# Routing of two expert layers in a five-stage model kernel: GpSimd takes choices, products and table rows, and ranks are handed on by halves

## The chip, the cores and the metric

The kernel runs on 1 core of one Trainium2 chip. The metric is the device time of one execution in microseconds (us); smaller is better. The engines are TensorE (PE, with weight loads PEld), VectorE (DVE), ScalarE (ACT), GpSimd (POOL) and SyncE (SP), which here only issues DMA. They run their own instruction streams and meet at semaphores.

## The reference, cut to what matters

The model is two layers of cross attention, a mixer (a state-space scan, then self attention) and an expert layer, on T = 2048 tokens of 256 values. The change is in the routing of the two expert layers, so that is what is shown. Layer 0 has 64 experts, 6 choices a token, a capacity of 128 tokens an expert; layer 1 has 64 experts in 8 groups, 8 choices a token, no capacity.

```python
# layer 0
scores = jax.nn.softmax(xf @ gate_w.T, axis=-1)
_, idx = jax.lax.top_k(scores + gate_b, K)            # K = 6
flat_e = idx.reshape(-1); order = jnp.argsort(flat_e); se = flat_e[order]
counts = jnp.bincount(flat_e, length=E); starts = jnp.cumsum(counts) - counts
pos = jnp.arange(T * K) - starts[se]                  # a token's rank in its expert
xb = jnp.zeros((E, CAP, D), xf.dtype).at[se, pos].set(xf[tok], mode='drop')
...
# layer 1
scores = jax.nn.sigmoid(x @ w_router); swb = scores + b_router
group_scores = jnp.sum(jax.lax.top_k(swb.reshape(..., 8, 8), 2)[0], axis=-1)
group_idx = jax.lax.top_k(group_scores, 4)[1]
masked_scores = jnp.where(mask, swb, 0.0)
topk_idx = jax.lax.top_k(masked_scores, 8)[1]
sort = jnp.argsort(idx_flat); x_sorted = x_flat[sort // TOPK]
```

Each layer then runs every expert's gated product on its tokens, and adds a shared expert that all tokens pass.

## The kernel before, in words

`stage_moe` is called for layer 0 (`capped`) and for layer 1. Each call has a block for routing (prefix `m0r_`, `m1r_`), and then a block for the experts (`m0x_`, `m1x_`), with a barrier between them. The tokens lie as 16 tiles of 128 partitions; a half is 8 tiles (`HN`).

The steps of the routing block, nearly all on DVE, each waiting for the one before:

1. `normed`: 16 normalised tiles into the ring `xr` (4 buffers), stored to memory by SP and turned by PE; `logits` follow on PE. The ring's buffer is free when its store has landed.
2. `chosen(0)`, `chosen(1)`: per half the scores, the best 6 or 8 experts (`MAX8`, `FIND_INDEX8`), their numbers as floats `topf`, and for each choice k a one-hot row `oh` (L1418, 128 x 8 x 64, one instruction).
3. ranks: PE multiplies every `oh` with a triangular matrix and with ones (L1299, 2 matmuls for each k and half, sums in `psl`, `pst`). It waits for `hs` of the first shared units, and signals once, at the end of both halves.
4. DVE runs the sum over 16 tiles (`before`, L1441, a chain) and adds `psl` into `sel` (L1442). Layer 1 adds the start of each expert's block (L1446 to L1453).
5. slots: for each half K products `oh * sel` (L1462) and a reduction (L1464). Between them DVE gates units of the shared expert (L1169), for which PE (`units`, L1154) makes the products and ACT the SiLU. In layer 0 seven units are made in this block, in layer 1 four. PE starts unit m only when `hs` of unit m - 2 is written (two PSUM buffers).
6. the table: for each token tile and choice, n = 0 to 95 or 127, a one-hot row `atp` of the slot (L1483), a row `atb` (the token's number at its expert or block; L1486 or L1488 on DVE, L1346 or L1352 and L1354 on ACT), and one matmul (L1313). `by_scalar(n)` says which `atb` ACT makes: in layer 0 two of three, in layer 1 one of three. A ring of 16 (`HQ`) joins them. ACT comes to its rows only after its last SiLU.
7. `tok` and `dest` are read from the table; the barrier; the experts start with indirect gathers on POOL.

POOL has nothing to do in the routing block. The order on each engine is that of the code.

## Time and profile before

| | us |
|---|---|
| median of 3 runs | 2326.88 (2324.38 to 2330.84) |
| the profiled execution | 2326.39 |
| its span | 2324.7 |
| routing of layer 0, by the trace | 829.7 to 925 |
| routing of layer 1, by the trace | 1650.6 to 1791.6 |

Busy shares over the whole span are PE 80%, DVE 67%, POOL 54%, ACT 45%. They are averages over stages with different limits: in both routing stretches POOL's row of the page's 40 slices is 0, and DVE's is at its highest. The page's chain that ended last follows the last stage's gathers and stores and names none of the routing lines, because it is followed back along one release at a time; the barrier behind each routing block makes all engines wait for it.

### The profile page before, as it was taken

The numbers are of one execution on the slowest core, as the hardware profiler recorded it, in microseconds if no ns is written. First come the engines' busy times: TensorE is split into PE (matmuls) and PEld (weight loads), VectorE is DVE, ScalarE is ACT, GpSimd is POOL, SyncE is SP. The second block draws the span as 40 slices with busy tenths as digits, with TensorE's granted clock in tenths as the row PEclk, the third lists the DMA queues.
The fourth block names the chain that finished last, engine by engine and source line by source line (L and its number), as shares of the span: only waits on it lengthen the run. The fifth ranks groups of instructions, "written<-read, shape, count | busy, mean of one in ns | idle before, by whom it ended". The sixth has DMA issues, their size and how long they took to land. (4 is left out here: it accounts for less than half of the span.)

```text
span 2324.7 us, 38548 instructions
## 1 busy us (share of the span) xinstructions
PE 1861.1 (80%) x11288; PEld 1296.8 (56%) x11289; DVE 1551.5 (67%) x3374; ACT 1037.6 (45%) x2965; POOL 1261.1 (54%) x1015
## 2 busy tenths in 40 slices
PE   6799968989898668999869999699727999999100
PEld 6478833343433243677648888588512888888000
DVE  7699829999999968333447777377688333333733
ACT  1576637666666323233157777343306333333000
POOL 2588617777777700788425555366101555554776
PEclk9699988999999977999989999899765999999555
DMA  9121013212121052899601110100411999998333
GB/s 288 35 95 53 8 51 129 97 49 92 55 88 58 0 171 60 224 296 253 153 10 37 33 34 25 30 2 2 144 51 37 284 288 283 285 283 272 109 116 103
DMA packets 163806, 272.06 MB, mean 117 GB/s; under 512 B 28722, under 2 KB 97300, under 8 KB 162708
## 3 DMA queue, kind: packets, MB, share of 16 engines
q1 hardware_dynamic: 130708, 199.72, 26.6%
q0 software_dynamic: 30464, 68.19, 11.3%
q10 hardware_dynamic: 2496, 2.44, 0.3%
q8 instruction: 70, 1.15, 0.2%
q14 instruction: 68, 0.56, 0.1%
HBM read 218.74 MB, written 51.53 MB: 116 GB/s over the span
## 5 line engine op out<-in xcount | busy, mean ns | idle before, releaser
L1009 POOL TENSOR_TENSOR b_h<-b_h,b_bcb 128x1024 f32<-128x1024 f32 x128 | 301.7, 2358 | 115.4 <-DVE b_h L1074 114.9
L1588 POOL DMA_INDIRECT m1x_xb<-scratch_xn,m_tok x192 | 182.4, 950 | 313.8 <-DVE m1x_yb L1785 157.1
L1074 DVE TENSOR_TENSOR_SCAN b_h<-b_dA,b_pbx 128x1024 f32<-128x1024 f32 x128 | 292.6, 2286 | 4.4
L822 PE MATMUL b_psy<-b_h,ident 128*128 128x512 f32 x512 | 247.1, 611 | 55.9 <-POOL b_h L1009 55.9
L1635 PE MATMUL m1x_psh<-m1x_xe,m1x_w 128*128 128x128 f32 x1536 | 209.0, 280 | 7.5 <-DMA m1x_w<-in_m_w 6.7
L822 PEld LDWEIGHTS b_psy<-b_h,ident 128*128 128x128 f32 x512 | 93.5, 192 | 191.5 <-POOL b_h L1009 104.2
L1772 DVE TENSOR_TENSOR m1x_hT<-m1x_sg,m1x_psh 128x128 f32<-128x128 f32 x192 | 55.3, 288 | 215.6 <-ACT m1x_sg L1722 215.6
L1635 PEld LDWEIGHTS m1x_psh<-m1x_xe,m1x_w 128*128 128x128 f32 x1536 | 188.1, 193 | 16.8 <-issue 11.6
L1958 POOL TENSOR_TENSOR x_s<-x_s,x_rs 128x1024 f32<-128x1024 f32 x64 | 121.1, 1893 | 126.5 <-DVE x_rs L2124 126.5
L956 ACT ACTIVATE b_dA<-b_delta,b_A 128x504 f32<-128x504 f32 x256 | 166.1, 705 | 52.4 <-DVE b_h L1074 49.9
L1068 DVE TENSOR_TENSOR b_pbx<-b_pdx,b_bcb 128x1024 f32<-128x1024 f32 x128 | 157.7, 1232 | 21.7 <-ACT b_pdx L939 15.0
L1614 POOL DMA_INDIRECT m1x_yg<-scratch_y,m_gslot x128 | 124.6, 973 | 53.6 <-issue 38.7
L1649 PE MATMUL m1x_psy<-m_w2all,m1x_hT 128*128 x384 | 129.5, 419 | 5.1 <-issue 2.8
L1588 POOL DMA_INDIRECT m0x_xb<-scratch_xn,m_tok x64 | 63.0, 984 | 123.5 <-POOLq L1237 104.3
L2076 ACT ACTIVATE x_s<-x_s,x_nm 128x256 f32<-128x256 f32 x256 | 126.7, 502 | 0.0
L1716 ACT ACTIVATE m1x_xe<-m1x_psx 128x256 f32<-128x256 f32 x192 | 73.6, 383 | 114.5 <-PE m1x_psx L1624 114.5
L597 DVE TENSOR_TENSOR a_prod<-a_psk,a_kg 128x1024 f32<-128x1024 f32 x96 | 111.3, 1216 | 13.2 <-POOL a_kg L424 12.8
L1847 DVE SCALAR_TENSOR_TENSOR X<-m1x_yg,m1x_wts,X 128x256 f32<-128x256 f32 x128 | 62.3, 488 | 82.1 <-DMA m1x_yg<-scratch_y,m_gslot 78.0
L1597 POOL DMA_INDIRECT scratch_y<-x_area,m_dest x64 | 101.0, 1578 | 25.7 <-issue 13.7
L549 ACT ACTIVATE a_prod<-a_prod 128x128 f32<-128x128 f32 x384 | 112.5, 299 | 2.3 <-DVE a_prod L597 2.3
L432 POOL TENSOR_TENSOR a_ol<-a_probs,a_kg 128x1024 f32<-128x1024 f32 x48 | 90.0, 1902 | 39.7 <-DVE a_probs L630 39.7
L1722 ACT ACTIVATE m1x_sg<-m1x_psh 128x128 f32<-128x128 f32 x192 | 53.2, 277 | 118.2 <-PE m1x_psh L1635 117.7
...
## 6 DMA issues: line engine op xcount, KB each, us to landing
m1x_w<-in_m_w SPq DMA_DIRECT2D x192, 256.0 KB, 4.3
...
scratch_y<-m1x_yb SPq DMA_DIRECT2D x192, 128.0 KB, 3.9
...
```

The source lines that it names most:

```text
L549: ins = a.activation(w, w, ACT.Copy, accum_out=raw[:, t % 2, b, j, h:h + 1])
L822: mm = pe.matmul(psy[:, k % 2, :], ident[:, :], h[:, u % HB, j, :], start=False, stop=(nq == NQ - 1 and j == CQ - 1))
L956: ins = a.activation(dA[:, u % DB, j, :].rearrange("p (b l) -> p b l", b=NB)[:, :, 1:S], dv, ACT.Exp, scale=A[:, c, n:n + 1])
L1009: q.tensor_tensor(hs, hs, bcb[:, 1, CQ * nq:CQ * nq + CQ], ALU.mult).then_inc(sem("hc"), 1)
L1068: v.tensor_tensor(pbx[:, :, :], bc(pdx[:, (NCH * g + c) % 2, None, :], [P, CQ, GT]), bcb[:, 0, CQ * nq:CQ * nq + CQ], ALU.mult).then_inc(s ...
L1074: v.tensor_tensor_scan(h[:, u % HB].rearrange("p j n -> p (j n)"), dA[:, u % DB].rearrange("p j n -> p (j n)"), pbx[:, :, :].rearrange("p ...
L1588: g.indirect_dma_start(out=xb[:, j, :], out_offset=None, in_=xn, in_offset=bass.IndirectOffsetOnAxis(ap=tok[:, b:b + 1], axis=0)).then_inc ...
L1614: g.indirect_dma_start(out=yg[:, u, k, :], out_offset=None, in_=y, in_offset=bass.IndirectOffsetOnAxis(ap=gslot[:, t, k:k + 1], axis=0)).t ...
L1635: mm = pe.matmul(psh[u][0:CW[n], n, :], w13[:, j, k, lo:lo + CW[n]], xe[:, u, k, :], start=(k == 0), stop=(k == KD - 1))
L1649: mm = pe.matmul(psyy[u][:, 0:D], hT[:, u, 0, :], w2all[:, bass.ds(b, 1), :].rearrange("p o d -> p (o d)"), start=True, stop=True)
L1958: g.tensor_tensor(half, half, bc(rs_[:, b % 2, 4 * h:4 * h + 4, None], [P, 4, SK]), ALU.mult).then_inc(sem("probs"), 1)
L2076: ins = a.activation(s[:, b % 2, hp, :], s[:, b % 2, hp, :], ACT.Exp, bias=nm[:, b % 2, hp:hp + 1], scale=ISC, accum_out=sm[:, b % 2, hp:h ...
```

## The change

- POOL makes the one-hots `oh` of half 0 (all k) and of half 1 for the last `OHG` choices (1 in layer 0, 2 in layer 1), one `tensor_scalar` of 128x64 for each tile and choice: 56 and 80 instructions. DVE makes the other choices of half 1 as before. `hot_wait` picks the semaphore.
- PE signals `ranks` after each half, and DVE's chain L1441 and the add into `sel` run by halves (`sel` counts to 2).
- POOL makes the products of half 0 (6 or 8 `tensor_tensor` of 128x512) into `prg`, while DVE makes those of half 1 first; then DVE reduces both. The order of halves on DVE is (1, 0).
- table: `by_pool(n)`: POOL makes `atp` for one n of three in layer 0 (32 instructions) and for every second n in layer 1 (64). ACT's share in layer 1 falls from every third to every fourth n. DVE skips what the others make; its semaphore becomes one counter.
- the gating of the shared units 0 and 1 on DVE moves ahead of `MAX8` of half 1.
- SP issues the shared expert's weights behind the first four stores of `xr`, not ahead of them; the ring `xr` has 8 buffers in layer 1.
- several buffers are laid over each other (`many`, `gp`).

```diff
-    R, XR = 16 if capped else 8, 4
+    R, XR = (16, 4) if capped else (8, 8)
...
+            OHG = 1 if capped else 2
+            def hot_wait(eng, n, k):
+                if n == 0:
+                    eng.wait_ge(rs("oh_pool"), k + 1)
+                elif k >= K - OHG:
+                    eng.wait_ge(rs("oh_pool"), K + k - (K - OHG) + 1)
+                else:
+                    eng.wait_ge(rs("oh"), k + 1)
             def by_scalar(n):
-                return n % 3 != 2 if capped else n % 3 == 2
+                return n % 3 != 2 if capped else n % 4 == 2
+            def by_pool(n):
+                return n % 3 == 1 if capped else n % 2 == 1
+            def by_vector(n):
+                return not (by_scalar(n) and by_pool(n))
...
-                    sp.dma_start(ws13[:, :, :, :], d[f"m{layer}_ws13"]).then_inc(rs("shared"), 16)
-                    sp.dma_start(ws2[:, :, :], d[f"m{layer}_ws2"]).then_inc(rs("shared"), 16)
                     for t in range(NT):
+                        if t == 4:
+                            sp.dma_start(ws13[:, :, :, :], d[f"m{layer}_ws13"]).then_inc(rs("shared"), 16)
+                            sp.dma_start(ws2[:, :, :], d[f"m{layer}_ws2"]).then_inc(rs("shared"), 16)
...
                         for k in range(K):
-                            pe.wait_ge(rs("oh"), K * n + k + 1)
+                            hot_wait(pe, n, k)
...
-                    mm.then_inc(rs("ranks"), 1)
+                        mm.then_inc(rs("ranks"), 1)
...
+                @block.gpsimd
+                def _(g):
+                    g.wait_ge(rs("weights"), W_ALL)
+                    for n in range(2):
+                        g.wait_ge(rs("topf"), n + 1)
+                        for k in range(K - OHG if n else 0, K):
+                            for t in range(HN * n, HN * n + HN):
+                                ins = g.tensor_scalar(oh[:, t, k, :], iota[:, :], topf[:, t, k:k + 1], None, ALU.is_equal)
+                            ins.then_inc(rs("oh_pool"), 1)
...
+                    if capped:
+                        g.wait_ge(rs("sel"), 2)
+                        g.wait_ge(rs("scores_stored"), 16)
+                    else:
+                        g.wait_ge(rs("slots"), 1)
+                    for k in range(K):
+                        g.tensor_tensor(prg[:, :, k, :], oh[:, 0:HN, k, :], sel[:, 0:HN, :], ALU.mult).then_inc(rs("products"), 1)
+                    g.wait_ge(rs("placed"), 1)
+                    for n in range(NT * K):
+                        if by_pool(n):
+                            if n >= HQ:
+                                g.wait_ge(rs("at_used"), n - HQ + 1)
+                            g.tensor_scalar(atp[:, n % HQ, :], lineh[:, 0:P], place[:, 0, n // K, n % K:n % K + 1], None, ALU.is_equal).then_inc(rs("at_pool"), 1)
...
-                    v.wait_ge(rs("ranks"), 1)
-                    for t in range(NT):
-                        step(v.tensor_tensor(before[:, t + 1, :], before[:, t, :], pst[:, t, :], ALU.add))
+                    for n in range(2):
+                        q = slice(HN * n, HN * n + HN)
+                        v.wait_ge(rs("ranks"), n + 1)
+                        for t in range(HN * n, HN * n + HN):
+                            step(v.tensor_tensor(before[:, t + 1, :], before[:, t, :], pst[:, t, :], ALU.add))
+                        v.tensor_tensor(sel[:, q, :], before[:, q, :], psl[:, q, :], ALU.add).then_inc(rs("sel"), 1)
...
-                    for n in range(2):
+                    for n in (1, 0):
                         q = slice(HN * n, HN * n + HN)
-                        for k in range(K):
-                            ins = v.tensor_tensor(pr[:, :, k, :], oh[:, q, k, :], sel[:, q, :], ALU.mult)
-                        step(ins)
-                        step(v.tensor_reduce(slotf[:, q, :], pr[:, :, :, :], AX_X, ALU.add))
+                        if n:
+                            hot_wait(v, 1, K - 1)
+                            for k in range(K):
+                                ins = v.tensor_tensor(pr[:, :, k, :], oh[:, q, k, :], sel[:, q, :], ALU.mult)
+                            step(ins)
+                        else:
+                            v.wait_ge(rs("products"), K)
+                        step(v.tensor_reduce(slotf[:, q, :], pr[:, :, :, :] if n else prg[:, :, :, :], AX_X, ALU.add))
```

DVE in layer 0, from the sum of the ranks to the slots, before (`m_hs` is the gating of a shared unit, `x_area` holds `before`, `sel` and the products):

```order
L1441 TENSOR_TENSOR x_area<-x_area,m0r_pst 128x64 x16
L1442 TENSOR_TENSOR x_area<-x_area,m0r_psl 128x1024
L1169 TENSOR_TENSOR m_hs<-m_sgs,m0r_psT 96x512
L1462 TENSOR_TENSOR x_area<-m0r_oh,x_area 128x8x64 x6
L1464 TENSOR_REDUCE m0r_slotf<-x_area 128x48
L1169 TENSOR_TENSOR m_hs<-m_sgs,m0r_pst 128x512
L1169 TENSOR_TENSOR m_hs<-m_sgs,m0r_psl 128x512
L1462 TENSOR_TENSOR x_area<-m0r_oh,x_area 128x8x64 x6
L1464 TENSOR_REDUCE m0r_slotf<-x_area 128x48
L1169 TENSOR_TENSOR m_hs<-m_sgs,m0r_pst 96x512
L1169 TENSOR_TENSOR m_hs<-m_sgs,m0r_psl 128x512
```

and the same place in the changed kernel:

```order
L1508 TENSOR_TENSOR x_area<-x_area,m0r_pst 128x64 x8
L1509 TENSOR_TENSOR x_area<-x_area,m0r_psl 128x512
L1508 TENSOR_TENSOR x_area<-x_area,m0r_pst 128x64 x8
L1509 TENSOR_TENSOR x_area<-x_area,m0r_psl 128x512
L1169 TENSOR_TENSOR m_hs<-m_sgs,m0r_psT 96x512
L1532 TENSOR_TENSOR x_area<-m0r_oh,x_area 128x8x64 x6
L1536 TENSOR_REDUCE m0r_slotf<-x_area 128x48
L1169 TENSOR_TENSOR m_hs<-m_sgs,m0r_pst 128x512
L1169 TENSOR_TENSOR m_hs<-m_sgs,m0r_psl 128x512
L1536 TENSOR_REDUCE m0r_slotf<-x_area 128x48
L1169 TENSOR_TENSOR m_hs<-m_sgs,m0r_pst 96x512
```

One of the two sets of six products has gone from DVE; the gating of the shared units stands where it stood, and the chain L1441 is in two parts.

POOL between the mixer and the experts of layer 0 goes from nothing to this (the second line of the block is a single set-up instruction):

```order
L1355 UNCONDITIONAL_BRANCH
L1363 ISA
L1363 TENSOR_SCALAR m0r_oh<-m0r_iota,m0r_topf 128x64 x56
L1372 TENSOR_TENSOR x_area<-m0r_oh,x_area 128x8x64 x6
L1378 TENSOR_SCALAR m0r_atp<-m0r_lineh,x_area 128x128 x32
```

These 94 instructions are new on POOL; in layer 1 they are 80, 8 and 64.

## Rows read from the trace of the kernel before

**Rows 1.** Busy us by stretch: length, PE, PEld, DVE, ACT, POOL, clock, DMA, GB/s.
```profile
903.10:925.00 21.90, 17.80 (x96) 9.96 (x96) 21.37 (x133) 16.48 (x60) 0.00 (x0) 0.53 0.00 1
1748.80:1791.60 42.80, 36.47 (x128) 13.38 (x128) 42.47 (x218) 37.58 (x84) 0.00 (x0) 0.50 0.00 1
```
**Rows 2.** Instructions in order of time, DVE, layer 0: start, us, [idle before].
```profile
859.99 0.20 DVE L1414 CAST m0r_topf<-m0r_topi 128x64 f32<-128x64 uint32 x1
...
880.32 4.05 DVE L1441 TENSOR_TENSOR x_area<-x_area,m0r_pst 128x64 f32<-128x64 f32 x16 [3.94 <-PE m0r_pst L1299]
...
886.27 3.69 DVE L1462 TENSOR_TENSOR x_area<-m0r_oh,x_area 128x512 f32<-128x512 bf16 x6
890.00 3.35 DVE L1464 TENSOR_REDUCE m0r_slotf<-x_area 128x48 f32<-128x3072 f32 x1
...
903.14 0.58 DVE L1483 TENSOR_SCALAR m0r_atp<-m0r_lineh,x_area 128x128 f16<-128x128 f16 x3
903.63 0.23 DVE L1486 TENSOR_SCALAR m0r_atb<-m0r_oh,m0r_tokf 128x64 f16<-128x64 bf16 x1
```
**Rows 3.** In order of time, PE, layer 0: first rank matmul, shared units 2, 3.
```profile
872.75 0.61 PE L1299 MATMUL m0r_psl<-m0r_oh,m0r_ltrib 128*128 128x512 bf16 x1 [7.28 <-DVE m_hs L1169]
...
880.05 3.60 PE L1154 MATMUL m0r_psT<-m_xnT,m_ws 128*96 128x512 f32 x8
885.74 3.67 PE L1154 MATMUL m0r_pst<-m_xnT,m_ws 128*128 128x512 f32 x8 [2.09 <-issue]
```
**Rows 4.** In order of time, ACT, layer 0, last SiLU and first table rows.
```profile
901.33 0.60 ACT L1163 ACTIVATE m_sgs<-m0r_psl 128x512 f32<-128x512 f32 x1 [2.84 <-PE m0r_psl L1154]
901.83 18.79 ACT L1346 ACTIVATE m0r_atb<-m0r_oh,m0r_tokf 128x64 f16<-128x64 bf16 x64
```
**Rows 5.** In order of time, DVE, layer 1, from the choices to the slots.
```profile
1685.65 0.20 DVE L1414 CAST m1r_topf<-m1r_topi 128x64 f32<-128x64 uint32 x1
1685.88 4.91 DVE L1418 TENSOR_TENSOR m_oh<-m1r_iota,m1r_topf 128x512 bf16<-128x512 f32 x8
...
1707.37 0.20 DVE L1414 CAST m1r_topf<-m1r_topi 128x64 f32<-128x64 uint32 x1
...
1718.28 4.05 DVE L1441 TENSOR_TENSOR m1r_before<-m1r_before,m1r_pst 128x64 f32<-128x64 f32 x16 [4.50 <-PE m1r_pst L1299]
...
1743.11 4.42 DVE L1464 TENSOR_REDUCE m1r_slotf<-m1r_pr 128x64 f32<-128x4096 f32 x1
```
**Rows 6.** Groups by line and form, both tables: count | busy us, mean ns.
```profile
L1488 DVE TENSOR_SCALAR m1r_atb<-m1r_lineh,m1r_place,m1r_tokf 128x192 f16<-128x192 f16 x86 | 29.4, 342 | 0.0
```
**Rows 7.** Groups by line and form, POOL over the whole span: count | busy us, mean ns.
```profile
L421 POOL TENSOR_TENSOR a_kra<-a_kg,a_sinq 128x96 f32<-128x96 f32 x16 | 6.3, 394 | 0.0
L2245 POOL TENSOR_TENSOR s_qblk<-s_qr,s_bm 128x512 f32<-128x512 f32 x16 | 16.6, 1040 | 1.3
L995 POOL TENSOR_TENSOR b_dx<-b_delta,b_xc 128x512 f32<-128x512 f32 x16 | 20.3, 1270 | 0.1
L325 POOL MEMSET a_clear<- 128x2176 f32 x1 | 1.9, 1911 | 0.3 <-POOLq L2653 0.3
L980 POOL MEMSET b_xcp<- 128x48 f32 x1 | 0.1, 148 | 15.8 <-POOLq L2544 15.8
```
**Rows 8.** In order of time, POOL, two small instructions with DVE off its inputs.
```profile
1212.21 0.76 POOL L1950 TENSOR_TENSOR x_qblk<-x_area,x_bm 128x128 f32<-128x128 f32 x2
```
**Rows 9.** In order of time, DVE and POOL at the start of the cross attention.
```profile
1192.77 1.42 DVE L2155 TENSOR_TENSOR X<-X,x_area 128x1024 f32<-128x1024 f32 x1
1194.11 1.42 DVE L2155 TENSOR_TENSOR X<-X,x_area 128x1024 f32<-128x1024 f32 x1
...
1194.41 1.38 POOL L1950 TENSOR_TENSOR x_qblk<-x_area,x_bm 128x128 f32<-128x128 f32 x1
...
1195.75 1.38 POOL L1950 TENSOR_TENSOR x_qblk<-x_area,x_bm 128x128 f32<-128x128 f32 x1
```
**Rows 10.** In order of time, DVE, layer 0, the ring of normalised tiles.
```profile
840.64 1.39 DVE L1370 TENSOR_SCALAR m0r_xr<-X,m0r_mean,m0r_rstd 128x256 f32<-128x256 f32 x4 [4.31 <-DMA scratch_xn<-m0r_xr]
```

More of the change, by code:

```diff
@@ L1189, in stage_moe @@
             if capped:
-                oh, sc = r.sb("oh", [P, NT, K, E], BF16), room("sc", NT, E)
+                oh = r.sb("oh", [P, NT, K, E], BF16)
+                many = cross.view(2 * HN * K * E + E)
+                sc, ex = (many[:, n * NT * E:(n + 1) * NT * E].rearrange("p (t e) -> p t e", e=E) for n in range(2))
+                before = many[:, (2 * HN * K - NT) * E:].rearrange("p (t e) -> p t e", e=E)
+                prg, pr = (many[:, n * HN * K * E:(n + 1) * HN * K * E].rearrange("p (t k e) -> p t k e", k=K, e=E) for n in range(2))
             slotf = r.sb("slotf", [P, NT, K])
             sel = room("sel", NT, E)
-            ex = room("ex", NT, E)
+            if not capped:
+                many = r.sb("many", [P, 2 * HN * K * E])
+                prg, pr = (many[:, n * HN * K * E:(n + 1) * HN * K * E].rearrange("p (t k e) -> p t k e", k=K, e=E) for n in range(2))
+                before = many[:, 0:(NT + 1) * E].rearrange("p (t e) -> p t e", e=E)
+                ex = many[:, HN * K * E:(HN * K + NT) * E].rearrange("p (t e) -> p t e", e=E)
+                gt8 = many[:, (HN * K + NT) * E:(HN * K + 2 * NT) * E].rearrange("p (t g k) -> p t g k", g=NGR, k=8)
+                gp = r.sb("gp", [P, HN, TOPG, NGR])
             row = r.sb("row", [P, 4, NT])
             top, topi, topf = r.sb("top", [P, NT, 8]), r.sb("topi", [P, NT, 8], U32), r.sb("topf", [P, NT, 8])
-            pr = room("pr", HN, K, E)
             ltrib, onesb = r.sb("ltrib", [P, P], BF16), r.sb("onesb", [P, P], BF16)
-            before = room("before", NT + 1, E)
             if not capped:
@@ L1222, in gate_up, with pool_count, vector_count @@
                 return [psT[n][:, :] for n in range(2)]
[L1224 to L1226 removed]
+            OHG = 1 if capped else 2
[6 more added lines that the diff above has]
+                    eng.wait_ge(rs("oh"), k + 1)
+            def by_scalar(n):
+                return n % 3 != 2 if capped else n % 4 == 2
[3 more added lines that the diff above has]
+                return not (by_scalar(n) and by_pool(n))
             def act_count(n):
                 return sum(by_scalar(i) for i in range(n))
+            def pool_count(n):
+                return sum(by_pool(i) for i in range(n))
+            def vector_count(n):
+                return sum(by_vector(i) for i in range(n))
             LOADS = [(gw[:, :, :], d[f"m{layer}_gw"]), (gb[:, :], d[f"m{layer}_gb"].partition_broadcast(P)),
@@ L1281, in units @@
                         if m > FIRST:
-                            pe.wait_ge(rs("sel"), 1)
+                            pe.wait_ge(rs("sel"), 2)
                         if m >= 2 and m != FIRST:
@@ L1403, in chosen @@
                             for k in range(TOPG):
-                                step(v.tensor_tensor(pr[:, :, k, 0:NGR], bc(iota[:, None, 0:NGR], NQ), bc(topf[:, q, k:k + 1], NQ), ALU.is_equal))
-                            step(v.tensor_reduce(gm[:, q, :], pr[:, :, 0:TOPG, 0:NGR].rearrange("p t k g -> p t g k"), AX_X, ALU.add))
+                                step(v.tensor_tensor(gp[:, :, k, :], bc(iota[:, None, 0:NGR], NQ), bc(topf[:, q, k:k + 1], NQ), ALU.is_equal))
+                            step(v.tensor_reduce(gm[:, q, :], gp[:, :, :, :].rearrange("p t k g -> p t g k"), AX_X, ALU.add))
                             step(v.tensor_tensor(sel[:, q, :].rearrange("p t (g k) -> p t g k", k=8), sel[:, q, :].rearrange("p t (g k) -> p t g k", k=8),
                                                  bc(gm[:, q, :, None], [P, HN, NGR, 8]), ALU.mult))
+                        for m in range(FIRST if n else 0):
+                            shared_gated(v, m, gate_up(m)[1])
                         for t in tiles:
@@ L1413, in chosen @@
                         step(ins)
-                        step(v.tensor_copy(topf[:, q, :], topi[:, q, :]))
-                        for m in range(FIRST if n else 0):
-                            shared_gated(v, m, gate_up(m)[1])
-                        for k in range(K):
+                        v.tensor_copy(topf[:, q, :], topi[:, q, :]).then_inc(rs("topf"), 1)
+                        v.wait_ge(rs("topf"), n + 1)
+                        for k in range(K - OHG if n else 0):
                             v.tensor_tensor(oh[:, q, k, :], bc(iota[:, None, :], NE), bc(topf[:, q, k:k + 1], NE), ALU.is_equal).then_inc(rs("oh"), 1)
@@ L1452, in _ @@
                         step(v.tensor_scalar(nb[:, 3, :], nb[:, 3, :], float(P), None, ALU.mult))
-                        step(v.tensor_tensor(sel[:, :, :], sel[:, :, :], bc(nb[:, 3:4, :], NE), ALU.add))
+                        v.tensor_tensor(sel[:, :, :], sel[:, :, :], bc(nb[:, 3:4, :], NE), ALU.add).then_inc(rs("slots"), 1)
+                        v.wait_ge(rs("slots"), 1)
                         for n in range(2):
@@ L1475, in _ @@
                         v.wait_ge(rs("block"), 1)
-                        step(v.tensor_copy(place[:, :, :, :], sloti[:, :, :, :]))
+                        v.tensor_copy(place[:, :, :, :], sloti[:, :, :, :]).then_inc(rs("placed"), 1)
+                        v.wait_ge(rs("placed"), 1)
                         v.tensor_scalar(far[:, :, :], place[:, 1, :, :], -1.0, None, ALU.mult).then_inc(rs("far"), 1)
@@ L1480, in _ @@
                             n = K * t + k
+                            if not by_vector(n):
+                                continue
                             if n >= HQ:
                                 v.wait_ge(rs("at_used"), n - HQ + 1)
-                            ins = v.tensor_scalar(atp[:, n % HQ, :], lineh[:, 0:P], place[:, 0, t, k:k + 1], None, ALU.is_equal)
+                            if not by_pool(n):
+                                ins = v.tensor_scalar(atp[:, n % HQ, :], lineh[:, 0:P], place[:, 0, t, k:k + 1], None, ALU.is_equal)
                             if not by_scalar(n):
```

22 lines of the change are left out of this document (13 added, 9 removed).

## The prediction

> **What bounds the kernel now.** I read first the busy time by stretch of the two tables [rows 1]: DVE is busy 21.37 of 21.90 us in layer 0 and 42.47 of 42.80 us in layer 1, POOL 0, and the clock is at its lower level (0.53 and 0.50, so 1.2 GHz), since PE has only small matmuls there. Then the instructions in order of time. In layer 0 [rows 2] the numbers of the choices of half 0 are ready at 860.2, DVE waits 3.94 us for PE until 880.3, and the table begins at 903.1. In layer 1 [rows 5] the same points lie at 1685.9 and 1718.3 (a wait of 4.50 us), and the last reduction starts at 1743.1, so that the slots are there at 1747.5. Between these points DVE hardly rests. It is the chain of the block, and the barrier behind it holds the experts back. So whatever DVE loses counts, unless PE, ACT or POOL ends later. I take the wall time from 829.7 to 925 and 1650.6 to 1791.6 as the only one that the change touches.
>
> **The price of a POOL instruction.** The trace has no POOL tensor_scalar. Its small tensor_tensors of 128x96 take 394 ns [rows 7]. Two of 128x128 take 0.76 us together [rows 8], some 0.37 us from start to start. From 128 to 512 elements with one input broadcast it goes to 1040 ns, a slope of 1.67 ns an element; so 64 elements with two inputs come to 0.26 us, and up to 0.35 us by the 128x96 row. From below stands a memset: 148 ns for 48 elements, and (1911 - 148) / 2128 = 0.83 ns an element, so 0.16 us for 64 and 0.21 us for 128. A tensor_scalar reads one tensor and a scalar for each partition; I take 0.25 us for 128x64 and 0.33 us for 128x128, near the tensor_tensors, because they read too. The ends 0.16 and 0.35 (and 0.21 and 0.45) go into the range. The products are dense on both sides, 1270 ns [rows 7].
>
> **DVE and POOL shut each other out.** At the start of the cross attention DVE has four tensor_tensors with two SBUF inputs beside POOL's small ones [rows 9]. Both go in step: DVE starts every 1.34 us (1192.77, 1194.11) and POOL too (1194.41, 1195.75), where the POOL instruction alone needs 0.37 us [rows 8]. DVE's 1024 elements stream for about 1.07 us, which leaves some 0.27 us for POOL's 0.37; so each holds the way for its own streaming part, about its distance less 0.1 us, and they alternate. For 128x64 choices I take 0.15 us held, for 128x128 0.23 us, for a product 1.13 us; DVE's 128x512 with two inputs holds 0.54 us. The Trainium skill (SBUF — State Buffer, Who interferes with whom) calls the pair of ports that DVE and GpSimd share an exclusive lock, taken by DVE instructions with two SBUF inputs or in a two-port mode such as a 16-bit tensor_scalar; by that rule the rows above agree, and the products here meet in the same way.
>
> **Layer 0, step by step.**
> Ring: DVE waited 4.31 us for the store of tile 0 [rows 10], which was queued behind the shared weights. With the stores ahead, tile 4 can be made at 836.3, where DVE ends its casts. PE then goes on at its 1.17 us a tile, so that tile 4 is turned 2.4 us earlier. Tile 8 waits for a store behind the weights, which land about 7 us after their issue as before (842.5), not later than PE wants it. Gain 2.4; it is 0 if the stores are late again. Choices of half 0 begin at 857.9.
> Choices: POOL needs 48 x 0.25 = 12 us. DVE's two score instructions cost it 0.9. DVE itself saves 3.7 us of one-hots and reaches the numbers of half 1 at 867.6 (it now waits for the shared units ahead of them, which end at 864.5 on ACT). Its five one-hots, 867.6 to 871.1, go in step with five of POOL's (0.54 + 0.15 each). POOL ends half 0 at 873.1 and the last 8 at 875.1. PE has the ranks of half 0 at 874.0. Those of half 1 take it 4.3 us for five k, at 0.43 us a matmul: PE waited between the k's, and from a wait of 7.28 us its first matmuls ran at the lower level [rows 3]. Then 0.6 more: 879.0, against 880.05, where unit 2 starts now [rows 3]. Gain 1.0, the ring's in it.
> Ranks to slots, counted from that unit's start: 23.1 us before. `sel` is ready at 2.9 (8 steps of 0.253 and a half add in place of 5.6). That gain is lost at once. Unit 2 must pass PE and ACT until 4.3, so DVE's products of half 1 start at 4.95. POOL began its own at 3.0 and has 4.4 left. In step at 0.54 + 1.13 = 1.67 a pair they take DVE to 12.9 and not 8.6. The reduction, 3.35 us [rows 2], ends at 16.3, the gating of units 3 and 4 at 17.5. Unit 5 needs unit 3's gating: PE 3.6 us each [rows 3], two of them to 24.2, SiLU, gating: slots at 25.8. So 2.7 us are lost here; POOL's products are hidden, and what is late is PE's shared units.
> Table: DVE does two `atp` and one `atb` for three n; before, the 32 rounds of three and one ran from 903.1 to 923.5, 0.635 us each. An `atp` is 0.16 of it (three in 0.58 us [rows 2], each 250 ns long). So 32 x 0.473 = 15.1 us. POOL's 32 rows at 0.33 are 10.6 us, so not the bound, and hold 0.23 each. DVE's own 0.13 us between short instructions covers most of it, which leaves 0.1, 3.2 in all. ACT still has 64 rows, 18.8 us [rows 4], from its last SiLU on: 24.9 + 18.8 = 43.7. DVE: 25.8 + 18.3 = 44.1. Before it was 43.4. Loss 0.7 in place of 2.7. Layer 0 in sum: 1.0 - 0.7 = 0.3 gained.
>
> **Layer 1.** The ring of 8 gains nothing, PE was the bound.
> Choices: 64 x 0.25 = 16 us and 1.6 behind DVE's score instructions: half 0 done at 1703.6. DVE is at 1704.5 where it was at 1707.6 [rows 5] (it saves 4.9, gates two units ahead, 1.2, and yields 0.5). Six one-hots in step with POOL to 1708.7, POOL's 16 done at 1711.2, PE one k later, 1712.1. Before: 1718.0. Gain 5.9.
> Ranks to slots, before 29.5 us. `sel` is 2.6 us earlier. Then POOL starts products at 6.0, DVE at 7.6 and 8.3. Six pairs of 1.67 and two of 0.6 end at 19.5, two reductions of 4.42 [rows 5] and a gating at 29.0. Gain 0.5; without the meeting on the ports it would be 7.8.
> Table: 1748.8 to 1790.2 for 128 n, 41.4 us; without 128 `atp` of 0.162 that leaves 0.24 for each of 86 `atb`. Now 64 `atp` and 96 `atb`: 33.4. The `atb` here, 342 ns for 192 elements with two operations [rows 6], goes at one element a cycle and leaves POOL its way; only `atp` meets it, 64 x 0.04 = 2.6. So 36.0, with POOL 21 us and ACT 32 pairs at 0.93, 30 us, behind it. Gain 5.4. Layer 1 in sum: 11.8.
>
> **Sum.** 0.3 + 11.8 = 12.1 us off the profiled execution's 2326.4. It stands 0.5 under the median of 2326.9, so I forecast 2314.8 for the median.
>
> **Rivals.**
> A, slower: a choice costs POOL 0.42 us or more. It has its place ahead of the ranks: 48 + 8 instructions in layer 0 and 64 + 16 in layer 1 stand before PE's last rank matmul. Each 0.01 us costs 0.5 and 0.8 us. From the forecast, 0.17 x 130 = 22 us: 2337. It decides from 0.35 us on. For it: an operand for each partition may cost what no row shows; against it: 0.26 us by the nearest slope.
> B, no change: a choice at 0.29 to 0.35, which is the 128x96 row itself: 2320 to 2328.
> C, the table eats its gain: every DVE instruction that falls on a POOL row waits for all of it. In layer 1, 64 x 0.23 = 14.7 in place of 2.6, in layer 0, 32 x 0.23 = 7.4 in place of 3.2: 2331.
> The Trainium skill's lock is held for the whole instruction (same page and section), which leans to C; rows 9, where POOL's share is less than its distance, lean against.
> D, much faster: the products don't shut each other out. Then layer 0 gets its slots at 21.4 and is bound by ACT, 4 us less, and layer 1 is 7.3 us less: 2303.5. Against it stand rows 9; for it, that DVE may be served first.
> E, one-input instructions go at the memset's price: 0.20 for a choice. Layer 0 gains 2 more, layer 1 about 2 (then DVE's own choices bound it): 2311.
> The Trainium skill (GPSIMD Engine Reference, Engine selection) says that one-input work on GpSimd is roughly at line rate and two-input work twice as slow as on VectorE; that is E's side.
>
> **How the numbers follow.** Forecast, with choices between 0.22 and 0.28 us, 0.37; E 0.13; D 0.15; B 0.18; C 0.07; A 0.10. Faster by over 0.3% (7 us; what a measurement of this kernel can tell from no change) hold the forecast, E and D, 0.65; within 0.3% B and most of C, 0.23; slower A and the rest of C, 0.12. The range runs from D's 2303.5, less 2.5 for a cheaper choice, 2301, to 2329; above it lie A and part of C, below it D together with E.
>
> **What would show it.** POOL's L1363 near 0.25 us from start to start; POOL ending half 1 after DVE; DVE's L1532 and POOL's L1372 at 1.6 to 1.7 us a pair; DVE waiting for PE's last shared unit ahead of L1541; the table of layer 1 at 36 us, that of layer 0 ending with ACT and DVE close together. I am wrong if L1363 is over 0.35 us, or if L1532 stays at 0.61.

## The result: 0.6% slower, and the profile after

| | before | after |
|---|---|---|
| median | 2326.81 us (2322.07 to 2330.84) | 2341.11 us (2336.04 to 2344.79) |
| ratio | | 1.0061, 95% interval 1.0047 to 1.0075 |
| the profiled execution | 2326.39 | 2344.05 |
| its span | 2324.7 | 2342.4 |

The forecast was 2314.8 us; the kernel became 14.3 us slower. Rival A is what happened.

To compare kernels I count a routing block from its first DVE instruction (the row statistics) to the first indirect gather of the experts behind it. Before, that is 829.73 to 926.11 and 1650.65 to 1792.83: 96.4 + 142.2 = 238.6 us. After it is 107.3 + 143.9 = 251.2 us, 12.6 more. The profiled executions differ by 17.7 us; the other 5.1 lie in stages whose code is the same, and the same kernel's runs spread by 9 us, so I explain only the 12.6. What makes the 5.1 stays open.

GpSimd's instructions of the routing of the changed kernel, groups by line and form: count, busy us, mean ns, idle time before.

```profile
L1378 POOL TENSOR_SCALAR m1r_atp<-m1r_lineh,m1r_place 128x128 f16<-128x128 f16 x64 | 39.3, 634 | 12.5 <-DVE m1r_place L1549 12.5
L1363 POOL TENSOR_SCALAR m_oh<-m1r_iota,m1r_topf 128x64 bf16<-128x64 f32 x80 | 36.7, 482 | 46.6 <-DVE m1r_topf L1480 46.6
L1363 POOL TENSOR_SCALAR m0r_oh<-m0r_iota,m0r_topf 128x64 bf16<-128x64 f32 x56 | 26.0, 489 | 36.3 <-DVE m0r_topf L1480 36.3
L1378 POOL TENSOR_SCALAR m0r_atp<-m0r_lineh,x_area 128x128 f16<-128x128 f16 x32 | 20.6, 662 | 16.7 <-DVE x_area L1541 16.7
L1372 POOL TENSOR_TENSOR m1r_many<-m_oh,m1r_sel 128x512 f32<-128x512 bf16 x8 | 11.2, 1438 | 6.6 <-DVE m1r_sel L1520 6.6
L1372 POOL TENSOR_TENSOR x_area<-m0r_oh,x_area 128x512 f32<-128x512 bf16 x6 | 8.6, 1459 | 4.3 <-issue 4.3
```

A choice costs 26.0 / 56 = 0.465 us from start to start, where I took 0.25; a table row 20.6 / 32 = 0.64 and 39.3 / 64 = 0.61, where I took 0.33; a product some 1.43 on average (1.12 while DVE has none, 1.57 while both have them).

What it does to layer 0, first DVE in order of time (start, us, idle before), the places of [rows 2]:

```profile
881.30 2.00 DVE L1508 TENSOR_TENSOR x_area<-x_area,m0r_pst 128x64 f32<-128x64 f32 x8 [11.73 <-PE m0r_pst L1335]
...
884.85 2.00 DVE L1508 TENSOR_TENSOR x_area<-x_area,m0r_pst 128x64 f32<-128x64 f32 x8 [0.83 <-PE m0r_pst L1335]
...
889.59 7.83 DVE L1532 TENSOR_TENSOR x_area<-m0r_oh,x_area 128x512 f32<-128x512 bf16 x6
...
908.72 0.69 DVE L1169 TENSOR_TENSOR m_hs<-m_sgs,m0r_pst 96x512 f32<-96x512 f32 x1 [3.33 <-ACT m_sgs L1163]
912.09 0.69 DVE L1169 TENSOR_TENSOR m_hs<-m_sgs,m0r_psl 128x512 f32<-128x512 f32 x1 [2.68 <-ACT m_sgs L1163]
```

then PE, rank matmuls of half 0 that follow GpSimd, and the shared unit 5, the places of [rows 3]:

```profile
876.86 0.61 PE L1335 MATMUL m0r_psl<-m0r_oh,m0r_ltrib 128*128 128x512 bf16 x1 [2.26 <-POOL m0r_oh L1363]
...
880.15 0.61 PE L1335 MATMUL m0r_psl<-m0r_oh,m0r_ltrib 128*128 128x512 bf16 x1 [2.26 <-POOL m0r_oh L1363]
...
884.65 3.60 PE L1154 MATMUL m0r_psT<-m_xnT,m_ws 128*96 128x512 f32 x8
...
901.67 6.31 PE L1154 MATMUL m0r_pst<-m_xnT,m_ws 128*96 128x512 f32 x8 [6.56 <-DVE m_hs L1169]
```

DVE waits 11.73 us for the first ranks. PE gets one k of choices every 3.30 us (eight instructions, so 0.41 us each while DVE stands still). Later PE itself waits 6.56 us for the gating of unit 3, and unit 5 then takes 6.31 us; [rows 3] have 3.60 for such a unit. The same unit 5 in the kernel before:

```profile
894.22 3.64 PE L1154 MATMUL m0r_pst<-m_xnT,m_ws 128*96 128x512 f32 x8 [1.38 <-DVE m_hs L1169]
```

Layer 1, DVE in order of time, the places of [rows 5]:

```profile
1731.62 2.00 DVE L1508 TENSOR_TENSOR m1r_many<-m1r_many,m1r_pst 128x64 f32<-128x64 f32 x8 [9.18 <-PE m1r_pst L1335]
...
1737.72 2.00 DVE L1508 TENSOR_TENSOR m1r_many<-m1r_many,m1r_pst 128x64 f32<-128x64 f32 x8 [3.38 <-PE m1r_pst L1335]
...
1743.47 1.33 DVE L1523 TENSOR_SCALAR m1r_many<-m1r_nb,m1r_iotab 128x64 f32<-128x64 f32 x2
...
1746.40 10.15 DVE L1532 TENSOR_TENSOR m1r_many<-m_oh,m1r_sel 128x512 f32<-128x512 bf16 x8
```

Before, one set of eight products on DVE alone:

```profile
1728.18 4.90 DVE L1462 TENSOR_TENSOR m1r_pr<-m_oh,m1r_sel 128x512 f32<-128x512 bf16 x8
```

And both tables, busy us by stretch as in [rows 1] (length, PE, PEld, DVE, ACT, POOL, clock, DMA share, GB/s):

```profile
912.93:934.05 21.12, 11.07 (x96) 5.96 (x96) 17.22 (x97) 16.65 (x61) 20.59 (x32) 0.52 0.01 2
1767.36:1807.20 39.84, 30.97 (x128) 11.33 (x128) 36.10 (x163) 30.73 (x64) 39.26 (x64) 0.50 0.00 1
```

In both, GpSimd has taken DVE's place as the engine that is busy nearly all the time.

### The profile page after: what moved, and what is told of

Read it like the earlier page. It is cut to its first block and busy times, and to the rows that moved or that the text cites. A ratio compares the mean times of both kernels' runs of the same rounds, so it can differ in the third digit from the quotient of the medians.

```text
span 2342.4 us, 38709 instructions
## 1 busy us (share of the span) xinstructions
PE 1857.4 (79%) x11288; PEld 1291.7 (55%) x11289; DVE 1536.1 (66%) x3259; ACT 1031.5 (44%) x2945; POOL 1404.2 (60%) x1261
## 5 line engine op out<-in xcount | busy, mean ns | idle before, releaser
L1674 POOL DMA_INDIRECT scratch_y<-x_area,m_dest x64 | 100.8, 1575 | 25.2 <-issue 14.3
L432 POOL TENSOR_TENSOR a_ol<-a_probs,a_kg 128x1024 f32<-128x1024 f32 x48 | 90.0, 1904 | 39.5 <-DVE a_probs L630 39.5
L489 PEld LDWEIGHTS a_psm<-ident,a_ol 128*128 128x128 f32 x768 | 91.4, 195 | 11.7 <-issue 10.0
```

## The experiments

The kernel before stood beside each of them; its median there was 2339 to 2349 us, so only ratios are compared. The two block lengths are from the profiled execution of each run. Three runs have one execution each and no interval.

| run | ratio to before | interval | layer 0 | layer 1 | blocks against before |
|---|---|---|---|---|---|
| before | | | 96.4 | 142.2 | |
| after | 1.0061 | 1.0047 to 1.0075 | 107.3 | 143.9 | +12.6 |
| e_changed (after, again) | 1.0037 | 1.0022 to 1.0051 | 106.4 | 143.7 | +11.5 |
| e_prices | | | 96.2 | 144.1 | +1.7 |
| e_choices_dve | 0.9947 | 0.9917 to 0.9977 | 89.9 | 136.7 | -12.0 |
| e_table_dve | 1.0065 | 1.0043 to 1.0087 | 107.8 | 146.5 | +15.8 |
| e_products_dve | 1.0017 | 0.9998 to 1.0035 | 102.3 | 142.0 | +5.7 |
| e_ring | | | 94.7 | 141.5 | -2.4 |
| e_nopool | 0.9961 | 0.9946 to 0.9975 | 90.1 | 138.3 | -10.2 |
| e_choices_some | 0.9960 | 0.9943 to 0.9977 | 100.5 | 133.7 | -4.4 |
| e_best1 | 0.9916 | 0.9891 to 0.9940 | 92.9 | 133.0 | -12.6 |
| e_best2 | 0.9923 | 0.9899 to 0.9947 | 87.5 | 132.8 | -18.2 |
| e_second | | | 89.2 | 133.1 | -16.3 |
| e_best3 | 0.9885 | 0.9864 to 0.9906 | 87.9 | 130.8 | -19.9 |

**The price list.** Is 0.465 us the instruction's own price, or made by contention with DVE?

```diff
+                @block.gpsimd
+                def _(g):
...
+                        for i in range(12):
+                            ins = g.tensor_scalar(atp[:, i, 0:64], iota[:, :], iotab[:, 0:1], None, ALU.is_equal)
...
+                            ins = g.tensor_scalar(atp[:, i, 0:16], iota[:, 0:16], iotab[:, 0:1], None, ALU.is_equal)
...
+                            ins = g.tensor_scalar(atp[:, i, 0:128], ltri[:, :], iotab[:, 0:1], None, ALU.is_equal)
...
+                            ins = g.tensor_scalar(atp[:, i, 0:64], iota[:, :], 3.0, None, ALU.is_equal)
...
+                            ins = g.tensor_copy(atp[:, i, 0:64], iota[:, :])
...
+                    g.wait_ge(rs("at", 0), 1)
```

> The kernel before, with a list of GpSimd instructions added in both routing blocks; nothing waits for them but the start of the table, by which they are long done. Each list is back to back: is_equal with a scalar per partition at 128x64, 128x16 and 128x128; in layer 1 the same with a constant in place of the scalar, a copy of 128x64, and a product of 128x512 (bf16 by broadcast f32). Then, beside VectorE's table rows, 128x64 in layer 0 and 128x128 f16 in layer 1. Theory P (the instruction's own price, about 0.30 us fixed and 2.5 ns an element): 0.46 us for 64 columns, 0.34 for 16, 0.62 for 128, whether VectorE works or rests, and the same within 0.05 beside the table. Rival Q (contention with VectorE): at most 0.30 us for 64 columns early in the block, where VectorE rests for two thirds of the time, and over 0.45 beside the table. Rival R (it is the operand for each partition that costs): the constant form takes 0.26 us or less, the other 0.46. The product alone: 1.04 to 1.27 us. Total as before, within 3 us.

GpSimd in order of time, layer 0, then layer 1, groups back to back:

```profile
839.02 5.75 POOL L1332 TENSOR_SCALAR m0r_atp<-m0r_iota,m0r_iotab 128x64 f16<-128x64 f32 x12 [18.21 <-DMA m_ws<-in_m_ws]
844.86 3.60 POOL L1335 TENSOR_SCALAR m0r_atp<-m0r_iota,m0r_iotab 128x16 f16<-128x16 f32 x12
848.55 7.79 POOL L1338 TENSOR_SCALAR m0r_atp<-m0r_ltri,m0r_iotab 128x128 f16<-128x128 f32 x12
902.35 3.33 POOL L1356 TENSOR_SCALAR m0r_pmb<-m0r_iota,m0r_iotab 128x64 bf16<-128x64 f32 x7 [46.01 <-DVE m0r_atp L1529]
...
1659.13 4.19 POOL L1341 TENSOR_SCALAR m1r_atp<-m1r_iota 128x64 f16<-128x64 f32 x12 [17.29 <-DMA m_ws<-in_m_ws]
1663.39 2.53 POOL L1344 CAST m1r_atp<-m1r_iota 128x64 f16<-128x64 f32 x12
1666.02 3.50 POOL L1347 TENSOR_SCALAR m1r_pmb<-m1r_iota,m1r_iotab 128x64 bf16<-128x64 f32 x8
1669.61 4.76 POOL L1350 TENSOR_TENSOR m1r_pm<-m1r_pmb,m1r_iota 128x512 f32<-128x512 bf16 x4
```

Divided by their counts: 64 columns 0.48 us (f16 out) and 0.44 (bf16 out), 16 columns 0.30, 128 columns 0.65, 64 with a constant 0.35 (f16 out), a cast of 64 0.21, a product of 128x512 1.19. Beside the table 64 columns, bf16 out, take 3.33 / 7 = 0.48, 0.04 more than early in the block, and 128 columns beside the table of layer 1 take 0.69. So P holds for most of it: about 0.25 to 0.30 us fixed and, from 64 to 128 columns, some 2.7 ns for each element. The operand per partition makes 0.13 us of it (0.48 against 0.35), somewhat over half of what R said. The is_equal costs more than twice a cast of the same size. This run has one execution, 2349.2 us, where a total within 3 us of the kernel before was expected; its blocks are 1.7 us longer.

A second thing stands in the same run: what GpSimd's product does to single instructions of DVE. DVE in order of time, layer 1:

```profile
1668.39 0.41 DVE L1415 TENSOR_SCALAR m1r_xr<-X,m1r_mean,m1r_rstd 128x256 f32<-128x256 f32 x1 [0.53 <-PE m1r_psT L1271]
1669.56 1.36 DVE L1415 TENSOR_SCALAR m1r_xr<-X,m1r_mean,m1r_rstd 128x256 f32<-128x256 f32 x1 [0.76 <-PE m1r_psT L1271]
1670.84 1.38 DVE L1433 TENSOR_SCALAR m1r_ex<-m1r_ex 128x512 f32<-128x512 f32 x1
1672.26 3.35 DVE L1434 RECIPROCAL m_sc<-m1r_ex 128x512 f32<-128x512 f32 x1
```

While the four products ran (1669.6 to 1674.4), a tensor_scalar with one tensor took 1.36 in place of 0.41 us, and the next 1.38 (0.42 before). The reciprocal kept its 3.35. The Trainium skill (SBUF — State Buffer, Who interferes with whom) has DVE's tensor_scalar in a two-port mode among those that wait for the shared ports, and by it the other engine is shut out for the whole instruction; these rows agree. The 1.3 us of L1523 in the changed kernel above (0.55 before), also beside GpSimd's products, fit this.

**The choices.**

```diff
-                                ins = g.tensor_scalar(oh[:, t, k, :], iota[:, :], topf[:, t, k:k + 1], None, ALU.is_equal)
...
-                        for k in range(K - OHG if n else 0):
+                        for k in range(K):
                             v.tensor_tensor(oh[:, q, k, :], ...
```

> The changed kernel with all choices made by VectorE again (12 and 16 instructions of 128x512); products and table rows stay on GpSimd, ranks stay in halves, the ring order stays. Theory P: the choices on GpSimd are what made the kernel slower. Layer 1: the ranks of half 1 end about 7 us earlier after the block's start; layer 0: about 8 us earlier, of which the shared units on TensorE may keep some back. In sum 12 to 15 us faster than the changed kernel: 2326 to 2329. If instead the loss lies in the products or the table, the gain is under 4 us: 2337 or more.

Measured: 0.9947, and blocks 24.6 us shorter than in the changed kernel, more than the 12 to 15 expected. In layer 0 DVE now starts on the first ranks at once, 869.87, where it had waited 11.73 us, and the products fare better as well:

```profile
869.87 2.00 DVE L1496 TENSOR_TENSOR x_area<-x_area,m0r_pst 128x64 f32<-128x64 f32 x8
...
876.05 3.69 DVE L1520 TENSOR_TENSOR x_area<-m0r_oh,x_area 128x512 f32<-128x512 bf16 x6
```

GpSimd's products there (shortest, median and longest in ns, first and last start):

```profile
L1360 POOL TENSOR_TENSOR x_area<-m0r_oh,x_area x6: 1154/1158/3470, 877.3 to 885.2; 128x512 f32<-128x512 bf16 x6
```

The first waits until DVE's six are done. So the choices alone turned a kernel that would have been 12 us faster into one that is 12 us slower. Layer 1 gave 7.2 of the 24.6, as expected, layer 0 17.4, twice of what was expected. Of these 17.4 us, 9.5 come ahead of TensorE's unit 2, 4.4 between it and the table, and 3.5 in the table: the choices also set how GpSimd's products met DVE's (below).

**The table.**

```diff
-                return n % 3 != 2 if capped else n % 4 == 2
+                return n % 3 != 2 if capped else n % 3 == 2
...
-                return n % 3 == 1 if capped else n % 2 == 1
+                return False
```

> The changed kernel with GpSimd out of the table: VectorE makes every atp row and ScalarE has its old share. Theory P: in layer 0 the table was bound by GpSimd's 32 rows of 0.65 us (21.0 us against 20.4 before), in layer 1 it took 39.5 us against 41.4. So 0.6 gained and 1.9 lost: 2342 to 2343. Rival: GpSimd's rows hold VectorE back in more than they save, then it is 3 us or more faster than the changed kernel: under 2338.

Measured: 1.0065, blocks 3.2 us longer than in the changed kernel (0.6 and 2.6). So GpSimd's rows did save, but only some 3 us, nearly all of it in layer 1. The sign for layer 0 isn't shown: 0.6 us is less than the 0.9 by which the changed kernel's own two profiled executions differ there.

**The products.**

```diff
-                    for k in range(K):
-                        g.tensor_tensor(prg[:, :, k, :], oh[:, 0:HN, k, :], sel[:, 0:HN, :], ALU.mult).then_inc(rs("products"), 1)
...
-                            v.wait_ge(rs("products"), K)
...
+                            for k in range(K):
+                                ins = v.tensor_tensor(prg[:, :, k, :], oh[:, q, k, :], sel[:, q, :], ALU.mult)
+                            step(ins)
```

> The changed kernel with all products on VectorE (two sets of 6 or 8 in place of one), choices and table rows as changed. Theory P with shared ports: a pair took 1.3 to 1.4 us, two products on VectorE alone 1.23, and VectorE's small instructions at the start waited 1.3 us for GpSimd in layer 1. So all products on VectorE cost nothing or gain up to 2 us: 2339 to 2341. Rival D (the engines do not shut each other out): 3.7 and 4.9 us more of work on VectorE's path, 2347 to 2350.

Measured: 1.0017, blocks 6.9 us shorter than in the changed kernel. D would have made them longer; it is out. The theory had the sign, but not the size in layer 0, 4.9 us: products on GpSimd are a loss in the changed kernel. The pair of 1.3 to 1.4 us in the expectation is an average over products that met and products that ran alone. In the changed kernel, line, count, shortest, median and longest ns, first and last start:

```profile
L1532 DVE TENSOR_TENSOR x_area<-m0r_oh,x_area x6: 678/1640/1648, 889.6 to 896.7; 128x512 f32<-128x512 bf16 x6
L1372 POOL TENSOR_TENSOR x_area<-m0r_oh,x_area x6: 1160/1604/1615, 887.7 to 894.7; 128x512 f32<-128x512 bf16 x6
```

Where both engines have products, DVE's start at 890.47, 892.04, 893.61 and 895.18, so a pair takes 1.57 us. Two products on DVE alone take 1.20 (3.69 us for six). So while both engines have nothing but products, sharing them loses.

**One part alone: the ring.**

> The kernel before with one part of the change alone: the stores of xr ahead of the shared weights, and a ring of 8 in layer 1. The numbers of half 0 come 1.5 to 2.4 us earlier in layer 0 (28.0 to 28.8 us after the block's start; 30.26 before), the block 94 to 95 us in place of 96.4; layer 1 within 0.5 us of 142.2. If the earlier numbers are lost again in the wait for the ranks, the block of layer 0 stays at 96 us.

The numbers of half 0 came at 28.16 us after the block's start (30.26 before), the block took 94.7 us. Of 2.1 us gained, 1.7 arrive. Layer 1 is 0.7 us shorter, where at most 0.5 was expected.

**Nothing on GpSimd.** The three edits above together.

> The changed kernel without any work on GpSimd in the routing: choices, products and table rows on VectorE; the ranks by halves, the gating ahead of MAX8 and the ring order are kept. By the traces so far the two routing blocks took 96.4 + 142.2 = 238.6 us before, 107.3 + 143.9 = 251.2 changed, 89.9 + 136.7 = 226.6 with choices on VectorE. Theory P: the gain of that run over before comes from halves, order and ring, and GpSimd's products and table rows add little: 90 to 92 + 138 to 139 = 228 to 231 us, 8 to 10 us faster than the kernel before (ratio 0.996). Rival: GpSimd's help is what made that run fast; then this one is within 4 us of the kernel before.

Measured 0.9961 and 228.4 us. The halves, the earlier gating of units 0 and 1, the order and the ring bring 10.2 us by themselves, with no GpSimd, so the rival is out. The ring alone has 2.4 of it; what the halves and the gating bring one by one was not separated.

**As much as GpSimd can hide.**

```diff
+            GH = 3 if capped else 4
...
+                    for k in range(K - GH, K):
+                        for t in range(HN):
+                            ins = g.tensor_scalar(oh[:, t, k, :], iota[:, :], topf[:, t, k:k + 1], None, ALU.is_equal)
...
+                        for k in range(K if n else K - GH):
```

> The changed kernel with GpSimd making only the choices it can finish while VectorE ranks half 1: the last 3 of 6 (layer 0) and the last 4 of 8 (layer 1) of half 0, and none of half 1. At 0.465 us an instruction that is 24 x 0.465 = 11.2 and 32 x 0.465 = 14.9 us, against some 10.5 and 20.5 us until the numbers of half 1. Theory P: no rank waits for GpSimd by more than 1 us; VectorE saves 3 x 0.62 and 4 x 0.61 us against the run with all choices on VectorE: blocks 88 to 90 + 134 to 135 us, 15 us faster than before (ratio 0.9935). Rival (GpSimd's choices slow VectorE down by contention): no gain over the run with all choices on VectorE, 226 us or more.

Layer 1 did as P says: 133.7 us, 3.0 less than with all choices on DVE. Layer 0 did not, 100.5 in place of 88 to 90. The choices are only a part of it: GpSimd in order of time, then DVE and PE:

```profile
853.15 14.05 POOL L1359 TENSOR_SCALAR m0r_oh<-m0r_iota,m0r_topf 128x64 bf16<-128x64 f32 x24 [36.66 <-DVE m0r_topf L1477]
...
872.18 2.00 DVE L1505 TENSOR_TENSOR x_area<-x_area,m0r_pst 128x64 f32<-128x64 f32 x8 [1.49 <-PE m0r_pst L1333]
...
876.92 9.53 DVE L1529 TENSOR_TENSOR x_area<-m0r_oh,x_area 128x512 f32<-128x512 bf16 x6
...
890.70 6.01 PE L1154 MATMUL m0r_pst<-m_xnT,m_ws 128*96 128x512 f32 x8 [8.25 <-DVE m_hs L1169]
```

24 choices took 0.585 us each, not 0.465: beside DVE at work a choice costs more than the 0.41 that it costs while DVE waits. So Q has a share after all, 0.05 to 0.17 us on average; in the changed kernel the eight choices that run beside DVE's six one-hots of layer 1 (1718.55 to 1722.37) take 0.79 us each. The larger part, though, is the products: 9.53 us for DVE's six in place of 3.69, PE waits 8.25 us for the gating behind them, and runs unit 5 in 6.01.

**A smaller share, and the products of layer 0.** Both have 2 and 4 choices k of half 0 on GpSimd, and one of six and three of eight table rows; the products of layer 1 are all on DVE in both. They differ in the products of layer 0 alone.

```diff
-                return n % 3 == 1 if capped else n % 2 == 1
+                return n % 6 == 1 if capped else n % 8 in (1, 4, 7)
```

> As the run before, with 2 of 6 and 4 of 8 choices of half 0 on GpSimd; products of layer 0 shared as changed, those of layer 1 all on VectorE (24.7 us from the last chain step to the last reduction against 26.4 in the run with shared products); GpSimd's table rows cut to one of six (16 rows, 10 us) and three of eight (48 rows, 30 us). Theory P: layer 0 table 19 us (ScalarE's 18.8 bound it) and layer 1 table 37 to 38 us, where TensorE's 128 matmuls at 0.289 us (37.0) are the bound; blocks 87 to 89 + 130 to 132 us, 18 to 21 us faster than before (ratio 0.9915). If the table is not bound so, it stays at 20 and 39.5: 4 us less gain.

> As the run before, but the products of layer 0 on VectorE too. If sharing them gains nothing (pairs of 1.4 us against 1.23 for two on VectorE), layer 0 is the same within 1 us. If VectorE's head start decides (in the run with choices on VectorE its six products took 3.69 us undisturbed, GpSimd's first one waited), it is 1 to 2.5 us slower than the run before in layer 0.

Measured: 0.9916 with blocks of 92.9 + 133.0 us, and 0.9923 with 87.5 + 132.8. In the profiled executions sharing the products costs 5.4 us of layer 0, where I had expected no difference or the opposite sign. The ratios, with intervals of 6 us to either side, neither show nor exclude that, and in both runs the profiled execution was the slowest of the four. Unit 5 on PE, in order of time, e_best1 and then e_best2:

```profile
888.68 6.57 PE L1154 MATMUL m0r_pst<-m_xnT,m_ws 128*96 128x512 f32 x8 [4.29 <-DVE m_hs L1169]
```

```profile
887.61 3.65 PE L1154 MATMUL m0r_pst<-m_xnT,m_ws 128*96 128x512 f32 x8 [1.38 <-DVE m_hs L1169]
```

The longer wait makes 2.9 us of it and the slower unit as much. But the length of the wait alone doesn't decide: behind shorter waits than the 3.32 us of e_second below, which left its unit at 3.64, these two were slow, unit 3 in e_ring and unit 5 in e_products_dve:

```profile
879.03 5.37 PE L1154 MATMUL m0r_pst<-m_xnT,m_ws 128*128 128x512 f32 x8 [2.08 <-issue]
```

```profile
896.35 5.22 PE L1154 MATMUL m0r_pst<-m_xnT,m_ws 128*96 128x512 f32 x8 [2.42 <-DVE m_hs L1169]
```

The granted clock between 901.67 and 908.00 in the changed kernel says why a unit takes 6.3 us and not 3.6: 0.57, near 1.2 GHz, where it was 1.00 between 884.65 and 895.00. In e_ring it was 0.68 during unit 3.

The table of layer 1 stayed at 39.5 us in e_best2, so that part of the expectation failed (the table of layer 0 took 18.8, as expected). What bound it is DVE, not PE as I had said:

```profile
1737.17:1776.71 39.54, 35.12 (x128) 13.31 (x128) 39.30 (x178) 30.72 (x64) 31.25 (x48) 0.50 0.00 1
```

80 x 0.162 + 96 x 0.24 = 36.0, so 48 rows of GpSimd cost DVE 3.3 us, 0.07 each. By the same sum it is 0.04 each for the 64 rows of the changed kernel (36.1 against 33.4).

**Who comes first.**

```diff
+                        g.wait_ge(rs("ahead"), 1)
...
+                                if k == 0:
+                                    ins.then_inc(rs("ahead"), 1)
```

> The run with shared products in layer 0, with one wait more: GpSimd starts its six products only when VectorE has finished its first one. Two explanations are open for the run with all choices on VectorE, where VectorE's six products took 3.69 us undisturbed and GpSimd's first one 3.47 us. H1, whoever works first keeps the way while its next instruction is ready: then VectorE's six products take 3.7 to 4.2 us here, GpSimd's first one over 3 us, TensorE waits under 2.5 us for unit 5 and runs it at 2.4 GHz (3.6 us), and layer 0 takes 87 to 89 us. H2, it was chance how the two fell in step: then they alternate as in the changed kernel, VectorE's six take 6 to 8 us, TensorE waits 4 us or more, unit 5 takes 6.3 to 6.6 us, and layer 0 takes 92 to 94 us.

Neither. GpSimd was held back further by the store of the scores, which landed at 876.5; DVE's six took 5.63 us, and layer 0 89.2:

```profile
874.50 5.63 DVE L1528 TENSOR_TENSOR x_area<-m0r_oh,x_area 128x512 f32<-128x512 bf16 x6
...
884.39 3.64 PE L1154 MATMUL m0r_pst<-m_xnT,m_ws 128*96 128x512 f32 x8 [3.32 <-DVE m_hs L1169]
...
876.50 8.00 POOL L1368 TENSOR_TENSOR x_area<-m0r_oh,x_area 128x512 f32<-128x512 bf16 x6 [13.76 <-DMA scratch_xn<-x_area]
```

DVE had worked for 2 us when GpSimd came, and was slowed all the same, so H1 does not hold as a rule. Nor does it in e_best1, where DVE was 1.5 us ahead and its six took 6.60 us. Why DVE kept the way in the run with all choices on DVE (3.69 us, though GpSimd came 1.2 us later) stays open. PE waited 3.32 us here and still ran unit 5 in 3.64.

**The version that beats both.**

```diff
+            GH = 2 if capped else 5
...
+                return n % 3 != 2 if capped else n % 16 in (2, 4, 8, 10, 14)
...
+                return n % 6 == 1 if capped else n % 2 == 1 and n % 16 != 15
```

> The changed kernel once more, as a reference on the same chip as the next one. Ratio to the kernel before 1.005 to 1.007; blocks 107 + 144 us.

> The run with all products on VectorE and 2 and 4 choices of half 0 on GpSimd had blocks of 87.5 + 132.8 us. This one gives GpSimd 5 of 8 choices of half 0 in layer 1 (40 x 0.465 = 18.6 us, within the 20.8 us until the numbers of half 1) and shares the table of layer 1 anew: GpSimd 56 rows (56 x 0.615 = 34.4 us), ScalarE 40 (37.4), VectorE 72 + 88 (72 x 0.162 + 88 x 0.24 + 56 x 0.07 for the meeting with GpSimd = 36.7), TensorE 37. So 0.6 us less ahead of the ranks and a table of 37.5 to 38.5 in place of 39.5: layer 1 at 130.5 to 132 us, layer 0 the same; ratio to the kernel before 0.9915. If the table's contention grows with GpSimd's rows by more than 0.07 us a row, layer 1 stays at 133.

The changed kernel again: 1.0037, blocks 106.4 + 143.7; a little below the expected ratio, the blocks as expected. e_best3: 0.9885, 2318.2 us beside 2343.4 us of the kernel before. Its blocks are 19.9 us shorter, 0.85%, a little less than the interval begins with (0.94%), so some of the gain is not explained by them. Both blocks came as expected (87.9 + 130.8 us). Its table of layer 1:

```profile
1732.45:1770.43 37.98, 27.25 (x128) 13.40 (x128) 35.12 (x163) 35.78 (x80) 34.44 (x56) 0.50 0.00 1
```

DVE, ACT and GpSimd are at 34 to 36 us, PE at 27. PE's 37 us, which I had called a floor twice, are none: the busy time of the same 128 matmuls was 36.5 before, 35.1 in e_best2, 31.0 in the changed kernel and 27.3 here. What sets it was not tested.

## Why the prediction was wrong, step by step

**What bounds the kernel**: right. Both blocks were DVE's (by [rows 1]; in the page's slices DVE stands at 6 to 8 tenths there and at 9 in the mixer, so the slices alone don't show it), and what I wrote of the barrier behind them holds: the change of the block lengths lies within the interval of the ratio in seven of the ten timed runs; in the other three (e_choices_some, e_best1, e_best3) the kernel did better than its profiled blocks by 5 to 7 us. For two of these the products of layer 0 may have met otherwise in the other executions; that can't be seen, since only the profiled execution has a trace, and it was the slowest of its run in both.

**The price of a POOL instruction** is the step that failed. I priced a tensor_scalar by tensor_tensors of the same size (0.25 and 0.33 us), with 0.35 and 0.45 as the upper ends. It measured 0.41 alone and 0.465 on average for a choice, 0.61 to 0.65 for a row; both lie beyond the range. The rows that I had were multiplications (394 ns for 128x96) and a memset, no comparison. The Trainium skill (GPSIMD Engine Reference, Engine selection), quoted for E, has one-input work roughly at line rate; 2.7 ns an element and 0.25 to 0.30 fixed are far from that, and the measurement decides. By A's own sum, 0.215 x 130 = 28 us on 2314.8, the kernel would be at 2342.8; it is at 2341.1. That they meet so closely is luck: the choices put both blocks 17.0 us behind the forecast, not 28 (6.3 and 10.7, up to the last rank). The rest of the blocks' 24.7 us is 5.6 in the two tables and 2.1 between ranks and slots.

**DVE and POOL shut each other out**: right in kind and nearly in size. A pair of products took 1.57 us, not 1.67. D is out, since DVE's set of products went from 3.69 to 7.83 us in layer 0 and from 4.90 to 10.15 in layer 1.

**Layer 0.** Ring: 2.3 us forecast as 2.4. Choices: unit 2 on PE starts 55.6 us after the block's start in place of 50.3, a loss of 5.3 where 1.0 was to be gained. Ranks to slots: 28.3 us; before 23.1, forecast 25.8. The mechanism was the one forecast, PE's units 5 and 6 behind late gating, but I gave unit 5 its 3.6 us; behind a wait of 6.56 it took 6.31. These 2.7 us are what is missing (28.3 against 25.8). Table: 21.1 us against 18.3 for DVE and 18.8 for ACT; GpSimd bound it. In sum -10.9 in place of +0.3.

**Layer 1.** Choices: the last ranks 72.4 us after the start in place of 67.6, a loss of 4.8 where 5.9 were to be gained. Ranks to slots: 0.9 us gained, 0.5 forecast. Table: DVE's own work was 36.1 us, forecast 36.0, so C is out (its `atp` took 284 ns on average, 266 before, and its `atb` 324, 342 before: only `atp` met GpSimd's rows, as forecast); but GpSimd's 64 rows at 0.61 are 39.3, where I had 21. Gain 2.2 in place of 5.4. In sum -1.7 in place of +11.8.

**The chances.** A had 0.10 and decided from 0.35 us on. The trace held no instruction of the kind, and the 128x96 row stood at my very upper end; a range for a price without a row should have reached beyond the dearest row near it, not up to it.
